# Placing TensorE's short matmuls between its long ones in the attention stage of a five-stage fp32 kernel

## The chip, the cores and the metric

The program runs on one core of a Trainium2 chip. The metric is the device time of one execution in microseconds; the kernel before was run three times. Hardware numbers in this text come from its profile.

## The reference, cut to what is computed

Five layers work in turn on x of shape (4, 512, 128): a gated feed-forward, a state-space mixer, the feed-forward again, a mixture of experts, attention with 8 heads, and the experts again. Each stands behind a layer norm and is added to x. The change touches attention alone:

```python
q = (x @ Wq + bq).reshape(Bsz, Tlen, NUM_HEADS, HEAD_DIM)      # 8 heads of 128
kv = x @ Wkv + bkv                                             # one k and one v for all heads
k, v = (kv[..., :HEAD_DIM], kv[..., HEAD_DIM:])
q = q + pe[None, None, :, :]                                   # after a transpose to (b, h, t, d)
k = k + pe[None, :, :]
scores = jnp.einsum('bhqd,bkd->bhqk', q, k) * scale
scores = jnp.where(causal[None, None, :, :], scores, jnp.finfo(scores.dtype).min)
probs = jax.nn.softmax(scores, axis=-1)
attn = jnp.einsum('bhqk,bkd->bhqd', probs, v)
return out @ Wo                                                # out: heads side by side
```

## The kernel before, in words

Each engine has its own instruction list, written out by hand, and the lists are tied together by counting semaphores. A layer is a phase that all engines enter together. Attention is phase 4. It goes over 4 blocks of 512 tokens (one sequence each) and, within a block, over 8 heads; the first three blocks are a loop (`Fori`), the last is written out.

An fp32 product is made of three matmuls on split operands (`mm3`, L227: hi x hi, hi x lo, lo x hi), which the engine runs at one column per cycle. Of one head, TensorE (`att_pe`, L1219 to L1344) does:

- `score(i, h)`, L1247: four row tiles of 128 queries, in the order 3, 2, 0, 1 (`ORDER`, L1200). Row tile r has three matmuls of 128(r+1) columns (L1261 to L1263) and a short one that adds the causal mask (L1264). The semaphore `s` goes up after tiles 3, 0 and 1.
- `values(i, h-1)`, L1279: probabilities of the head before, times v, 12 matmuls of 512, 384, 256 and 128 columns (L229 to L231). It waits for `pt_lo` 3g+3, the third low part of the transposed probabilities.
- `q_proj(i, h+2)`, L1239: three matmuls of 512 columns for the queries two heads on. In head 6 it is `k_proj` of the next block, in head 7 the next block's first `q_proj`; in the last block both are left out.
- `out_proj(i, h-2)`, L1292: three matmuls of 512 columns, none in heads 0 and 1.
- `turn(i, h)`, L1268: ten transposes of 128x128 of this head's probabilities (L1276), in the order of `PT_UNITS` (L1207): tile 2 (two transposes), tiles 1 and 3 (four), tile 0 (four). The semaphore `pt` goes up after each of the three. Before them it waits for `p` (all exponentials) and for `pn`: 2 normalised row tiles for the first unit, 4 for the others.

After head 7 come `v_proj` of the next block, `out_proj`(6), `values`(7), `q_proj`(1) and `score` of the next block's head 0, and `out_proj`(7). Head 0 of the loop therefore has no `score` or `values` in front.

ScalarE (`att_act`, L1346) does for each head: four exponentials with row sums (`p`, L1369), the copy of `values` and its high part (L1376, L234), three high parts `pt_hi` of the transposes (L1389), a high part of q. VectorE (`att_dve`, L1410): two reciprocals and four normalisations (L1447, L1451), `q32` out of the projection's bank (L1434), then first `pt_lo`, second `pt_lo`, the minimum of row tile 3 of the next head (L1440), third `pt_lo`, and the minima of tiles 2, 0 and 1. The minimum of tile 3 waits for one `s` of that head, those of tiles 2 and 0 for two, that of tile 1 for three. GpSimd makes the low parts of q, k, v and of the heads' outputs.

Of the kernel before, what the change touches and what calls it, by code (L numbers as in the profile page):

```python
# [1 line left out]

# [5 lines left out]
P = 128  # L17
# [7 lines left out]
HEADS = 8  # L25
# [34 lines left out]
def program(nc, d):  # L60
    ctx = ExitStack()
    with ctx:
# [12 lines left out]
        xn_hi = sb("xn_hi", [P, NT], F32R)  # L75
        xn_lo = sb("xn_lo", [P, NT], F32R)
# [42 lines left out]
        with ExitStack() as layer:  # L119
            lb = keeper(layer)  # L120
            ah, al = lb("ah", [P, NA], F32R), lb("al", [P, NA], F32R)
# [23 lines left out]
            with ExitStack() as s:  # L145
                fb = keeper(s)
                xb_hi, xb_lo = fb("xb_hi", [P, T], F32R), fb("xb_lo", [P, T], F32R)
                k_hi, k_lo = fb("k_hi", [P, T], F32R), fb("k_lo", [P, T], F32R)
# [3 lines left out]
                q_hi, q_lo = fb("q_hi", [P, 2, T], F32R), fb("q_lo", [P, 2, T], F32R)  # L152
                p32 = fb("p32", [P, 4, T])
                pt_hi, pt_lo = fb("pt_hi", [P, 3, T], F32R), fb("pt_lo", [P, 3, T], F32R)
                o_hi, o_lo = fb("o_hi", [P, 2, T], F32R), fb("o_lo", [P, 2, T], F32R)
# [5 lines left out]
        ps = ctx.enter_context(nc.psum_tensor("ps", [P, 8, T], F32))  # L161
# [62 lines left out]
        def cut(b):  # L224
            return slice(b * T, (b + 1) * T)

        def mm3(pe, out, w_hi, w_lo, x_hi, x_lo, start, stop):  # L227

            pe.matmul(out, w_hi, x_hi, start=start, stop=False, skip_group_check=True)  # L229
            pe.matmul(out, w_hi, x_lo, start=False, stop=False, skip_group_check=True)  # L230
            return pe.matmul(out, w_lo, x_hi, start=False, stop=stop, skip_group_check=True)  # L231

        def split_hi(act, hi, full):
            return act.activation(hi, full, ACT.Identity)  # L234
# [967 lines left out]
        def scores_at(r):  # L1202
            bank, lo = S_AT[r]
            return ps[:, bank, lo:lo + P * (r + 1)]
# [5 lines left out]
        def pt_at(kb):  # L1210
            bank, lo = PT_AT[kb]
            return ps[:, bank, lo:lo + T - P * kb]
# [4 lines left out]
            return ps[:, bank, lo:lo + n]  # L1217

        def att_pe(pe, L):  # L1219
            def k_proj(i, blk, first=False):  # L1220
                if not first:
                    pe.wait_ge(*A("q32", 8 * i - 2))
                w = slice(A_K, A_K + P)
                mm3(pe, ps[:, 5, :], ah[:, w], al[:, w], xn_hi[:, blk], xn_lo[:, blk], True, True).then_inc(A["kp"], 1)

            def v_proj(i, x_hi, x_lo, first=False):
                if not first:
                    pe.wait_ge(*A("xb_lo", i))
                    pe.wait_ge(*A("p", 32 * i - 3))
                w = slice(A_V, A_V + P)  # L1230
                for t in range(4):
                    tt = slice(t * P, (t + 1) * P)
                    out = ps[:, 0, tt]
                    pe.matmul(out, x_hi[:, tt], ah[:, w], start=True, stop=False, skip_group_check=True)
                    pe.matmul(out, x_hi[:, tt], al[:, w], start=False, stop=False, skip_group_check=True)
                    last = pe.matmul(out, x_lo[:, tt], ah[:, w], start=False, stop=True, skip_group_check=True)
                last.then_inc(A["vp"], 1)

            def q_proj(i, blk, h):  # L1239
                if h == 0:  # L1240
                    pe.wait_ge(*A("k32", i + 1))
                else:
                    pe.wait_ge(*A("q32", 8 * i + h))
                w = slice(A_Q + h * P, A_Q + (h + 1) * P)
                mm3(pe, ps[:, 5, :], ah[:, w], al[:, w], xn_hi[:, blk], xn_lo[:, blk], True, True).then_inc(A["qp"], 1)

            def score(i, h, first=False):  # L1247
                g = 8 * i + h
                if h == 0:
                    pe.wait_ge(*A("k_lo", i + 1))  # L1250
                    pe.wait_ge(*A("v32", i + 1))
                pe.wait_ge(*A("q_lo", g + 1))
                for k, r in enumerate(ORDER):
                    if not first and r != 0:
                        pe.wait_ge(*A("p", 4 * g - 4 + {3: 1, 2: 3, 1: 4}[r]))
                        if r == 1:
                            pe.wait_ge(*A("pt_lo", 3 * g - 2))
                    n = P * (r + 1)
                    q = slice(r * P, n)
                    out = scores_at(r)  # L1260
                    pe.matmul(out, q_hi[:, h % 2, q], k_hi[:, 0:n], start=True, stop=False, skip_group_check=True)  # L1261
                    pe.matmul(out, q_hi[:, h % 2, q], k_lo[:, 0:n], start=False, stop=False, skip_group_check=True)  # L1262
                    pe.matmul(out, q_lo[:, h % 2, q], k_hi[:, 0:n], start=False, stop=False, skip_group_check=True)  # L1263
                    last = pe.matmul(out[:, r * P:n], idr[:, :], maskr[:, :], start=False, stop=True, skip_group_check=True)  # L1264
                    if r != 2:
                        last.then_inc(A["s"], 1)

            def turn(i, h):  # L1268
                g = 8 * i + h
                pe.wait_ge(*A("p", 4 * g + 4))  # L1270
                pe.wait_ge(*A("pt_lo", 3 * g))
                for tiles, _, _, need in PT_UNITS:
                    pe.wait_ge(*A("pn", 4 * g + need))
                    for kb in tiles:
                        for r in range(kb, 4):
                            last = pe.transpose(pt_at(kb)[:, (r - kb) * P:(r - kb + 1) * P], p32[:, r, kb * P:(kb + 1) * P], ident)  # L1276
                    last.then_inc(A["pt"], 1)

            def values(i, h):  # L1279
                g = 8 * i + h  # L1280
                if h == 0:
                    pe.wait_ge(*A("v_lo", i + 1))
                pe.wait_ge(*A("o32", g))
                pe.wait_ge(*A("pt_lo", 3 * g + 3))
                for kb in range(4):
                    part, lo = PT_PART[kb]
                    n = T - kb * P
                    last = mm3(pe, ps[:, 6, kb * P:T], v_hi[:, kb, :], v_lo[:, kb, :], pt_hi[:, part, lo:lo + n],
                               pt_lo[:, part, lo:lo + n], kb == 0, kb == 3)
                last.then_inc(A["o"], 1)  # L1290

            def out_proj(i, h):  # L1292
                pe.wait_ge(*A("o_lo", 8 * i + h + 1))
                if h == 0:
                    pe.wait_ge(*A("x_new", i))
                w = slice(A_O + h * P, A_O + (h + 1) * P)
                mm3(pe, ps[:, 7, :], ah[:, w], al[:, w], o_hi[:, h % 2, :], o_lo[:, h % 2, :], h == 0, h == HEADS - 1)\
                    .then_inc(A["y"], 1)

            def heads(i, last):  # L1300
                blk, following = bass.ds(i * T, T), bass.ds((i + 1) * T, T)
                for h in range(HEADS):
                    if h:
                        score(i, h)
                        values(i, h - 1)
                    if h < HEADS - 2:
                        q_proj(i, blk, h + 2)
                    elif h == HEADS - 2 and not last:
                        k_proj(i + 1, following)
                    elif not last:  # L1310
                        q_proj(i + 1, following, 0)
                    if h >= 2:
                        out_proj(i, h - 2)
                    turn(i, h)
                if not last:
                    v_proj(i + 1, xb_hi, xb_lo)
                out_proj(i, HEADS - 2)
                values(i, HEADS - 1)
                if not last:
                    q_proj(i + 1, following, 1)  # L1320
                    score(i + 1, 0)
                out_proj(i, HEADS - 1)

            def first_kv(step):

                if step == 0:
                    pe.wait_ge(a_lo, 1)
                    pe.wait_ge(*L("centred", 1))
                    pe.wait_ge(*L("xn_lo", 1))
                    v_proj(0, xn_hi[:, 0:T], xn_lo[:, 0:T], True)  # L1330
                else:
                    pe.wait_ge(*L("normed", 2))
                    k_proj(0, cut(0), True)

            ln_pe(pe, L, first_kv)
            pe.wait_ge(*A("mask", 2))
            banks_free(pe, L)
            q_proj(0, cut(0), 0)
            q_proj(0, cut(0), 1)
            score(0, 0, True)  # L1340
            pe.wait_ge(*L("xn_lo", NB))
            with pe.Fori(0, NB - 1) as i:
                heads(i, False)
            heads(NB - 1, True)  # L1344
# [425 lines left out]
```

## Time and profile before

| | us |
|---|---|
| runs of the kernel before | 1946.06, 1946.1, 1943.2 |
| median | 1946.06 |
| span of the profiled execution | 1940.6 |
| attention stage in it | about 1219 to 1461 |

The profile has one record per instruction. PE is TensorE's matmuls, PEld its weight loads; DVE is VectorE, ACT ScalarE, POOL GpSimd. Starts and durations are in us from the start of the span. A matmul's end is modelled. A row that begins with L and a number is named by the line of the kernel; `ps<-k_hi,q_hi` reads: written to `ps`, the moving operand `k_hi`, the stationary one `q_hi`. "x10" means that ten records of the same kind stand in one row.

### The profile page before, as it was taken

How to read it: one execution, taken by the hardware profiler on the slowest of the kernel's cores; microseconds unless marked ns; L12 is line 12 of the kernel's file. 1: busy time of each engine (PE TensorE's matmuls, PEld its weight loads, DVE VectorE, ACT ScalarE, POOL GpSimd, SP SyncE). 2: the span in 40 equal slices, each digit the busy share in tenths (PEclk: the TensorE clock that was granted, in tenths of full speed). 3: DMA queues.
4: the chain of work that ended last, by engine and by line, in shares of the span. 5: the costliest groups of instructions: out<-in, count | busy, mean ns of one | idle time of the engine just before them, and what ended most of it. 6: DMA issues, size and time to landing. Idle time of an engine off the chain costs nothing.

```text
span 1940.6 us, 26739 instructions
## 1 busy us (share of the span) xinstructions
PE 1710.9 (88%) x7108; PEld 1270.5 (65%) x7108; DVE 1322.9 (68%) x2019; ACT 972.8 (50%) x1864; POOL 910.7 (47%) x786
## 2 busy tenths in 40 slices
PE   6997566666668997899999999899998899999999
PEld 3775322222226774688888887788885688888887
DVE  4555699999985556655555556777784655555565
ACT  3344634333334334455555554677783455555554
POOL 3001057445441003466666665434432466666666
PEclk8998768888889997999999999999997899999999
DMA  2000000000000001000010000000000000010001
GB/s 103 1 0 1 0 0 1 0 0 0 1 0 7 1 1 41 17 27 27 27 32 27 27 27 11 1 1 0 0 1 17 11 27 27 27 32 27 27 27 38
DMA packets 27793, 31.14 MB, mean 16 GB/s; under 512 B 3211, under 2 KB 26211, under 8 KB 27363
## 3 DMA queue, kind: packets, MB, share of 16 engines
q1 hardware_dynamic: 27747, 30.58, 5.2%
q8 instruction: 22, 0.36, 0.1%
q14 instruction: 24, 0.20, 0.0%
HBM read 29.52 MB, written 1.05 MB: 16 GB/s over the span
## 4 chain that ended last, share of the span: by engine, by line
PE 63%; issue 3%; DVE 3%; POOL 3%; ACT 1%; POOLq 0%; DVEq 0%; ACTq 0%
PE ps L229 17%; PE ps L230 16%; PE ps L231 16%; PE ps L914 4%; PE ps L1276 2%; POOL m_hc L837 2%; PE ps L1261 1%; PE ps L1263 1%; PE ps L1262 1%; PE ps L1264 0%; DVE r_t L1126 0%; POOL e_lo L237 0%; PE ps L251 0%; PE ps L264 0%; PE ps L258 0%
## 5 line engine op out<-in xcount | busy, mean ns | idle before, releaser
L237 POOL TENSOR_TENSOR e_lo<-e_h,e_hi 128x512 fp32r<-128x512 f32 (+1 forms) x368 | 479.4, 1303 | 313.3 <-ACT e_hi L234 313.3
L1157 DVE TENSOR_TENSOR e_p<-e_s,ps 128x512 f32<-128x512 f32 x352 | 242.1, 688 | 285.9 <-PE ps L231 195.4
L979 ACT ACTIVATE e_s<-ps 128x512 f32<-128x512 f32 (+1 forms) x368 | 220.6, 599 | 392.7 <-PE ps L231 392.6
L627 PE MATMUL ps<-m_hc,const 128*128 128x512 f32 x256 | 183.2, 806 | 113.6 <-POOL m_hc L837 105.4
L230 PE MATMUL ps<-xn_lo,eh 128*128 128x512 f32 x704 | 279.1, 397 | 0.0
L229 PE MATMUL ps<-xn_hi,eh 128*128 128x512 f32 x704 | 278.7, 396 | 0.0
L837 POOL TENSOR_TENSOR m_hc<-m_h,m_c 128x512 f32<-128x512 f32 x128 | 181.1, 1419 | 204.0 <-DVE m_h L793 164.7
L1166 DVE TENSOR_TENSOR e_h<-e_p,ps 128x512 f32<-128x512 f32 x352 | 242.3, 688 | 49.7 <-DVE e_p L1157 18.1
L231 PE MATMUL ps<-xn_hi,el 128*128 128x512 f32 x704 | 274.9, 390 | 0.0
L234 ACT ACTIVATE e_hi<-e_h 128x512 fp32r<-128x512 f32 (+1 forms) x368 | 229.6, 624 | 24.0 <-DVE e_h L1070 21.7
L793 DVE TENSOR_TENSOR_SCAN m_h<-ln_t,ln_c 128x512 f32<-128x512 f32 x128 | 237.8, 1858 | 0.5 <-ACT ln_t L701 0.5
L237 POOL TENSOR_TENSOR xn_lo<-ln_c,xn_hi 128x512 fp32r<-128x512 f32 (+1 forms) x24 | 34.2, 1427 | 325.8 <-ACT xn_hi L234 325.7
L627 PEld LDWEIGHTS ps<-m_hc,const 128*128 128x128 f32 x256 | 48.0, 230 | 207.8 <-POOL m_hc L837 195.4
L229 PEld LDWEIGHTS ps<-xn_hi,eh 128*128 128x128 f32 x704 | 132.7, 189 | 32.0 <-DVE e_p L1157 1.3
L230 PEld LDWEIGHTS ps<-xn_lo,eh 128*128 128x128 f32 x704 | 132.7, 189 | 31.4
L231 PEld LDWEIGHTS ps<-xn_hi,el 128*128 128x128 f32 x704 | 132.9, 189 | 30.9
L701 ACT ACTIVATE ln_t<-m_raw,neg_a 128x512 f32<-128x512 f32 x128 | 90.6, 719 | 121.9 <-DVE m_h L793 112.4
L229 PE MATMUL ps<-e_hi,eh 128*128 128x512 f32 x352 | 139.5, 396 | 1.9 <-POOL e_lo L237 1.9
L231 PE MATMUL ps<-e_hi,el 128*128 128x512 f32 x352 | 140.1, 398 | 0.0
L914 PE MATMUL ps<-rwt,eh 128*128 128x512 f32 x352 | 137.2, 390 | 1.4 <-ACT rwt L1000 1.4
L230 PE MATMUL ps<-e_lo,eh 128*128 128x512 f32 x352 | 136.3, 387 | 0.0
L229 PE MATMUL ps<-hid_hi,wh 128*128 128x512 f32 x288 | 122.2, 424 | 7.2 <-DVE hid_lo L237 6.2
(242 smaller groups left out, 3392.2 us busy)
## 6 DMA issues: line engine op xcount, KB each, us to landing
e_raw<-in_experts SPq DMA_DIRECT2D x88, 192.0 KB, 2.3
e_raw<-in_pick SPq DMA_DIRECT2D x88, 64.0 KB, 2.0
w_raw<-in_ffn SPq DMA_DIRECT2D x1, 1280.0 KB, 10.4
a_raw<-in_attn SPq DMA_DIRECT2D x1, 1152.0 KB, 5.2
w_raw<-in_ffn SPq DMA_DIRECT2D x1, 1024.0 KB, 7.8
out<-x SPq DMA_DIRECT2D x4, 256.0 KB, 2.4
x<-in_x SPq DMA_DIRECT2D x1, 768.0 KB, 4.6
w_raw<-in_ffn SPq DMA_DIRECT2D x1, 512.0 KB, 5.8
```

Of the source, the lines that this page charges most:

```text
L229: pe.matmul(out, w_hi, x_hi, start=start, stop=False, skip_group_check=True)
L230: pe.matmul(out, w_hi, x_lo, start=False, stop=False, skip_group_check=True)
L231: return pe.matmul(out, w_lo, x_hi, start=False, stop=stop, skip_group_check=True)
L234: return act.activation(hi, full, ACT.Identity)
L237: return eng.tensor_tensor(lo, full, hi.bitcast(F32), ALU.subtract)
L627: pe.matmul(ps[:, 4 + m, :], ident, m_hc[:, q % DEEP, :], start=(n == 0), stop=(n == DS - 1), skip_group_check=True).then_inc(M["y_sum"], 1)
L793: dve.tensor_tensor_scan(m_h[:, q % DEEP, :], m_da[:, q % DEEP, :], m_db[:, q % DEEP, :], 0.0, ALU.mult, ALU.add).then_inc(M["h"], 1)
L837: pool.tensor_tensor(m_hc[:, q % DEEP, :], m_h[:, q % DEEP, :], m_c[:, n % 2, :], ALU.mult).then_inc(M["hc"], 1)
L914: pe.matmul(ps[:, 6 + j % 2, :], eh[:, c, 3, :], rwt[:, cut(b)], start=True, stop=True).then_inc(S["spread"], 1)
L979: act.activation(e_s[0:rows_, buf, :], ps[0:rows_, 4, :], ACT.Silu).then_inc(S["silu"], 1)
L1157: dve.tensor_tensor(e_p[0:rows_, buf % 2, :], e_s[0:rows_, buf, :], ps[0:rows_, 5, :], ALU.mult).then_inc(S["gated"], 1)
L1166: dve.tensor_tensor(e_h[:, j % 4, :], e_p[:, j % 2, :], ps[:, 6 + j % 2, :], ALU.mult).then_inc(S["weighted"], 1)
```

## The change

`score` is written anew: the three products of tile 0 are placed between those of tile 3, then the two causal matmuls follow, then tile 2, then tile 1. `s` goes up after tiles 3, 2 and 1. `k_proj`, `q_proj` and `out_proj` are taken apart into single matmuls (`product`), and the transposes are placed between them: two projection products, transpose, third projection product, transpose, output product, transpose, output product, transpose, output product, and then the other six. The order of the transposes is now tile 2 (two), tile 3, tile 1 (three), tile 0 (four), with `pt` going up after the second, sixth and tenth as before. The waits for `p`, `pt_lo` and `pn` 2 stand behind the second projection product, the wait for `pn` 4 behind the second output product. The other engines' programs are unchanged.

```diff
+        def product(pe, k, out, w_hi, w_lo, x_hi, x_lo, start, stop):
+
+            return pe.matmul(out, w_lo if k == 2 else w_hi, x_lo if k == 1 else x_hi, start=start and k == 0,
+                             stop=stop and k == 2, skip_group_check=True)
...
-                for k, r in enumerate(ORDER):
-                    if not first and r != 0:
-                        pe.wait_ge(*A("p", 4 * g - 4 + {3: 1, 2: 3, 1: 4}[r]))
-                        if r == 1:
-                            pe.wait_ge(*A("pt_lo", 3 * g - 2))
...
-                    if r != 2:
-                        last.then_inc(A["s"], 1)
...
+                if not first:
+                    pe.wait_ge(*A("p", 4 * g - 1))
+                for k in range(3):
+                    part(3, k)
+                    part(0, k)
+                causal(3).then_inc(A["s"], 1)
+                causal(0)
+                for k in range(3):
+                    part(2, k)
+                causal(2).then_inc(A["s"], 1)
+                if not first:
+                    pe.wait_ge(*A("p", 4 * g))
+                    pe.wait_ge(*A("pt_lo", 3 * g - 2))
+                for k in range(3):
+                    part(1, k)
+                causal(1).then_inc(A["s"], 1)
...
-                    if h < HEADS - 2:
-                        q_proj(i, blk, h + 2)
-                    elif h == HEADS - 2 and not last:
-                        k_proj(i + 1, following)
-                    elif not last:
-                        q_proj(i + 1, following, 0)
-                    if h >= 2:
-                        out_proj(i, h - 2)
-                    turn(i, h)
...
+                    projection(h, 0)
+                    projection(h, 1)
+                    pe.wait_ge(*A("p", 4 * g + 4))
+                    pe.wait_ge(*A("pt_lo", 3 * g))
+                    pe.wait_ge(*A("pn", 4 * g + 2))
+                    turn(i, h, 2, 2)
+                    projection(h, 2)
+                    turn(i, h, 2, 3).then_inc(A["pt"], 1)
+                    output(h, 0)
+                    turn(i, h, 3, 3)
+                    output(h, 1)
+                    pe.wait_ge(*A("pn", 4 * g + 4))
+                    turn(i, h, 1, 1)
+                    output(h, 2)
+                    turn(i, h, 1, 2)
+                    turn(i, h, 1, 3).then_inc(A["pt"], 1)
+                    for r in range(3):
+                        turn(i, h, 0, r)
+                    turn(i, h, 0, 3).then_inc(A["pt"], 1)
```

## Rows read from the trace of the kernel before

**Rows 1.** The page: the span, and busy time by engine.
```profile
span 1940.6 us, 26739 instructions
PE 1710.9 (88%) x7108; PEld 1270.5 (65%) x7108; DVE 1322.9 (68%) x2019; ACT 972.8 (50%) x1864; POOL 910.7 (47%) x786
```
**Rows 2.** Table by stretches: length, busy by engine with counts, PEclk, DMA share, GB/s.
```profile
1239.00:1280.00 41.00, 41.00 (x271) 37.66 (x270) 33.52 (x86) 32.42 (x84) 15.19 (x13) 1.00 0.01 2
```
**Rows 3.** Timeline of weight loads, one head (start, duration, what).
```profile
1244.83 0.19 PEld L1262 LDWEIGHTS ps<-k_lo,q_hi 128*128 128x128 f32 x1
...
1245.29 0.19 PEld L1264 LDWEIGHTS ps<-maskr,idr 128*128 128x128 f32 x1
1245.52 0.19 PEld L1261 LDWEIGHTS ps<-k_hi,q_hi 128*128 128x128 f32 x1
1245.63 0.19 PEld L1262 LDWEIGHTS ps<-k_lo,q_hi 128*128 128x128 f32 x1
1245.81 0.19 PEld L1263 LDWEIGHTS ps<-k_hi,q_lo 128*128 128x128 f32 x1
1245.98 0.19 PEld L1264 LDWEIGHTS ps<-maskr,idr 128*128 128x128 f32 x1
...
1246.95 0.19 PEld L1264 LDWEIGHTS ps<-maskr,idr 128*128 128x128 f32 x1
1247.16 0.19 PEld L229 LDWEIGHTS ps<-pt_hi,v_hi 128*128 128x128 f32 x1
...
1249.40 0.19 PEld L231 LDWEIGHTS ps<-xn_hi,al 128*128 128x128 f32 x1
```
**Rows 4.** Timeline of PE: the ten transposes ahead of that head's score.
```profile
1243.73 1.25 PE L1276 MATMUL ps<-const,p 128*128 128x128 f32 x10
```
**Rows 5.** Timeline of DVE over the same head.
```profile
1245.22 0.69 DVE L237 TENSOR_TENSOR pt_lo<-ps,pt_hi 128x512 fp32r<-128x512 f32 x1 [0.23 <-ACT pt_hi L1389]
1245.83 0.68 DVE L1440 TENSOR_REDUCE st<-ps 128x1 f32<-128x512 f32 x1
1246.42 0.68 DVE L237 TENSOR_TENSOR pt_lo<-ps,pt_hi 128x512 fp32r<-128x512 f32 x1
...
1248.71 0.82 DVE L1451 TENSOR_SCALAR p<-p,st 128x512 f32<-128x512 f32 x2
...
1249.63 0.55 DVE L1451 TENSOR_SCALAR p<-p,st 128x128 f32<-128x128 f32 x2
...
1252.04 0.69 DVE L237 TENSOR_TENSOR pt_lo<-ps,pt_hi 128x512 fp32r<-128x512 f32 x1 [0.23 <-ACT pt_hi L1389]
```
**Rows 6.** Timelines of PE and DVE, first score of block 2.
```profile
1343.00 0.22 PE L1264 MATMUL ps<-maskr,idr 128*128 128x128 f32 x1
...
1344.03 0.27 PE L1264 MATMUL ps<-maskr,idr 128*128 128x128 f32 x1
...
1344.34 1.09 DVE L1440 TENSOR_REDUCE st<-ps 128x1 f32<-128x384 f32 x3 [0.39 <-PE ps L1264]
```
**Rows 7.** Timeline of PE: transposes of heads 1, 0 (block 2) and 6 (last block).
```profile
1236.70 1.46 PE L1276 MATMUL ps<-const,p 128*128 128x128 f32 x10
...
1347.55 0.44 PE L1276 MATMUL ps<-const,p 128*128 128x128 f32 x2 [1.34 <-DVE p L1451]
1348.21 1.09 PE L1276 MATMUL ps<-const,p 128*128 128x128 f32 x8 [0.22 <-DVE p L1451]
...
1446.95 1.39 PE L1276 MATMUL ps<-const,p 128*128 128x128 f32 x10
```
**Rows 8.** Timelines of DVE and PEld: first and last of the 28 places.
```profile
1233.26 0.68 DVE L237 TENSOR_TENSOR pt_lo<-ps,pt_hi 128x512 fp32r<-128x512 f32 x1
1234.00 0.19 PEld L229 LDWEIGHTS ps<-pt_hi,v_hi 128*128 128x128 f32 x1
...
1449.77 0.68 DVE L237 TENSOR_TENSOR pt_lo<-ps,pt_hi 128x512 fp32r<-128x512 f32 x1
1450.57 0.19 PEld L229 LDWEIGHTS ps<-pt_hi,v_hi 128*128 128x128 f32 x1
```

More of the change, by code:

```diff
@@ L1219, in att_pe, with k_proj @@
         def att_pe(pe, L):
-            def k_proj(i, blk, first=False):
-                if not first:
+            def k_proj(i, blk, k, first=False):
+                if k == 0 and not first:
                     pe.wait_ge(*A("q32", 8 * i - 2))
                 w = slice(A_K, A_K + P)
-                mm3(pe, ps[:, 5, :], ah[:, w], al[:, w], xn_hi[:, blk], xn_lo[:, blk], True, True).then_inc(A["kp"], 1)
+                mm = product(pe, k, ps[:, 5, :], ah[:, w], al[:, w], xn_hi[:, blk], xn_lo[:, blk], True, True)
+                if k == 2:
+                    mm.then_inc(A["kp"], 1)
             def v_proj(i, x_hi, x_lo, first=False):
@@ L1237, in v_proj, with q_proj @@
                 last.then_inc(A["vp"], 1)
-            def q_proj(i, blk, h):
-                if h == 0:
+            def q_proj(i, blk, h, k):
+                if k == 0 and h == 0:
                     pe.wait_ge(*A("k32", i + 1))
-                else:
+                elif k == 0:
                     pe.wait_ge(*A("q32", 8 * i + h))
                 w = slice(A_Q + h * P, A_Q + (h + 1) * P)
-                mm3(pe, ps[:, 5, :], ah[:, w], al[:, w], xn_hi[:, blk], xn_lo[:, blk], True, True).then_inc(A["qp"], 1)
+                mm = product(pe, k, ps[:, 5, :], ah[:, w], al[:, w], xn_hi[:, blk], xn_lo[:, blk], True, True)
+                if k == 2:
+                    mm.then_inc(A["qp"], 1)
             def score(i, h, first=False):
@@ L1252, in score @@
                 pe.wait_ge(*A("q_lo", g + 1))
-                for k, r in enumerate(ORDER):
-                    if not first and r != 0:
-                        pe.wait_ge(*A("p", 4 * g - 4 + {3: 1, 2: 3, 1: 4}[r]))
-                        if r == 1:
-                            pe.wait_ge(*A("pt_lo", 3 * g - 2))
[L1258 to L1264, printed above, removed]
-                    if r != 2:
-                        last.then_inc(A["s"], 1)
@@ L1268, in turn, with part @@
[L1268 to L1277, printed above, removed]
+                def part(r, k):
+                    q = slice(r * P, (r + 1) * P)
+                    x_lo, y_lo = (k == 2), (k == 1)
+                    pe.matmul(scores_at(r), (q_lo if x_lo else q_hi)[:, h % 2, q], (k_lo if y_lo else k_hi)[:, 0:P * (r + 1)],
+                              start=(k == 0), stop=False, skip_group_check=True)
@@ new lines, in causal @@
+                def causal(r):
+                    return pe.matmul(scores_at(r)[:, r * P:(r + 1) * P], idr[:, :], maskr[:, :], start=False, stop=True, skip_group_check=True)
+                if not first:
[7 more added lines that the diff above has]
+                    part(2, k)
@@ L1279, in values, with turn @@
+                causal(2).then_inc(A["s"], 1)
[5 more added lines that the diff above has]
+                causal(1).then_inc(A["s"], 1)
+            def turn(i, h, kb, r):
+                return pe.transpose(pt_at(kb)[:, (r - kb) * P:(r - kb + 1) * P], p32[:, r, kb * P:(kb + 1) * P], ident)
             def values(i, h):
@@ L1290, in values, with out_proj, projection, output @@
                 last.then_inc(A["o"], 1)
-            def out_proj(i, h):
-                pe.wait_ge(*A("o_lo", 8 * i + h + 1))
-                if h == 0:
+            def out_proj(i, h, k):
+                if k == 0:
+                    pe.wait_ge(*A("o_lo", 8 * i + h + 1))
+                if k == 0 and h == 0:
                     pe.wait_ge(*A("x_new", i))
                 w = slice(A_O + h * P, A_O + (h + 1) * P)
-                mm3(pe, ps[:, 7, :], ah[:, w], al[:, w], o_hi[:, h % 2, :], o_lo[:, h % 2, :], h == 0, h == HEADS - 1)\
-                    .then_inc(A["y"], 1)
+                mm = product(pe, k, ps[:, 7, :], ah[:, w], al[:, w], o_hi[:, h % 2, :], o_lo[:, h % 2, :], h == 0, h == HEADS - 1)
+                if k == 2:
+                    mm.then_inc(A["y"], 1)
             def heads(i, last):
                 blk, following = bass.ds(i * T, T), bass.ds((i + 1) * T, T)
+                def projection(h, k):
+                    if h < HEADS - 2:
+                        q_proj(i, blk, h + 2, k)
+                    elif h == HEADS - 2 and not last:
+                        k_proj(i + 1, following, k)
+                    elif not last:
+                        q_proj(i + 1, following, 0, k)
+                def output(h, k):
+                    if h >= 2:
+                        out_proj(i, h - 2, k)
                 for h in range(HEADS):
+                    g = 8 * i + h
                     if h:
@@ L1305, in heads @@
                         values(i, h - 1)
-                    if h < HEADS - 2:
-                        q_proj(i, blk, h + 2)
-                    elif h == HEADS - 2 and not last:
-                        k_proj(i + 1, following)
-                    elif not last:
-                        q_proj(i + 1, following, 0)
-                    if h >= 2:
-                        out_proj(i, h - 2)
-                    turn(i, h)
+                    projection(h, 0)
[17 more added lines that the diff above has]
+                    turn(i, h, 0, 3).then_inc(A["pt"], 1)
                 if not last:
                     v_proj(i + 1, xb_hi, xb_lo)
-                out_proj(i, HEADS - 2)
+                for k in range(3):
+                    out_proj(i, HEADS - 2, k)
                 values(i, HEADS - 1)
                 if not last:
-                    q_proj(i + 1, following, 1)
+                    for k in range(3):
+                        q_proj(i + 1, following, 1, k)
                     score(i + 1, 0)
-                out_proj(i, HEADS - 1)
+                for k in range(3):
+                    out_proj(i, HEADS - 1, k)
             def first_kv(step):
@@ L1332, in first_kv @@
                     pe.wait_ge(*L("normed", 2))
-                    k_proj(0, cut(0), True)
+                    for k in range(3):
+                        k_proj(0, cut(0), k, True)
             ln_pe(pe, L, first_kv)
@@ L1337, in att_pe @@
             banks_free(pe, L)
-            q_proj(0, cut(0), 0)
-            q_proj(0, cut(0), 1)
+            for h in range(2):
+                for k in range(3):
+                    q_proj(0, cut(0), h, k)
             score(0, 0, True)
```

## The prediction

> **What bounds the kernel now.** I read the page first for the size of things: the span is 1940.6 us and TensorE is busy 88% of it [rows 1]. Only the attention stage is edited, some 240 us from 1219 to 1461. The table by stretches then shows that in 41 us of its steady part PE is busy for 41.00 us at full clock [rows 2]. Read alone, this says that TensorE's own work sets the time. It has to be checked, because the end of a matmul is modelled and a matmul stretched by a wait also shows as busy.
>
> So the third view is the timeline of one head by its weight loads, which are the better clock: each load starts when the matmul before it starts. In [rows 3], a long matmul (512 columns, L below) takes 0.23 us: 1245.29 to 1245.52. A short one (128 columns, S below) takes 0.11 us in a run of its own kind: the ten transposes start at 1243.73 [rows 4] and the first score starts with the load at 1244.83 [rows 3], so 1.10 us for ten. Now the same rows at `values`: its first load is at 1247.16, while the last causal matmul, whose load is at 1246.95, began at about 1247.07 (a 256-column one of 0.12 us runs before it), when an unhindered load would have started. PE lost 0.09 us there, and the "busy" record hides it. What was late? VectorE's timeline [rows 5]: the third `pt_lo` runs from 1246.42 to 1247.10, and the load starts 0.06 after its end (0.12 in the last block, below). The chain before it is gapless: second `pt_lo` 1245.22, minimum of row tile 3 at 1245.83, third `pt_lo` 1246.42, paces 0.61 and 0.59. In [rows 8] the first and the last of the 28 such places (7 heads of 4 blocks) read the same way: 1233.26 + 0.68 then 1234.00; 1449.77 + 0.68 then 1450.57. So a steady head is a loop of two parts: from `values` to the sixth transpose PE is the bound, from there to the next `values` it is ScalarE and VectorE, with PE 0.09 us behind that. The head takes 6.82 us (second `pt_lo` at 1245.22 and one head later at 1252.04, [rows 5]).
>
> **The change, part by part.**
>
> **1. Shorts between longs: no gain.** The meant saving is that the load of an S hides behind an L. A short streams in well under 0.11 us, so its 0.11 is the load of the next weights. The kernel before already holds an S between two Ls: the causal matmul between 512- and 384-column scores. It starts with the load at 1245.52. The next load starts at 1245.63 (that of the second 384-column product), and then the 384s come at 1245.81 and 1245.98, 0.17 each [rows 3]. From 1245.52 to 1245.81 is 0.29 for S plus a 384; less 0.17 or 0.18, the S still costs 0.11. Its own load was hidden behind the L, but the load of the L behind it can only begin when the S begins, and lasts 0.11. An S costs 0.11 whatever stands before it. The matmuls, their shapes and number are unchanged, so this part is 0. Bounds: -0.055 us for each S with an L on both sides (three in a score, four in a block of transposes), and 0.
>
> The Trainium skill, "TensorE: Matmul & The Clock Gate", section "Step-by-step: what each phase is for", speaks for the change: it says that the engine's reorder window pulls weight loads ahead of matmuls in flight. The trace agrees for one load ahead, and shows none pulled two ahead. Were the rule enough by itself, the seven shorts would give back what rival B below counts.
>
> **2. Score order: the signal for row tile 3 comes later.** Before, `s` for tile 3 is raised by the fourth matmul of the score (3 L, causal), now three products of tile 0 lie in front: 3 x 0.11 = 0.33 us later. By load clock the score starts at 1244.83 and the causal matmul at 1245.52; it would start at 1245.85. Where VectorE was idle, its minimum started 0.04 after the end of the causal record (1344.03 + 0.27, then 1344.34, [rows 6]); behind an L that record is 0.22 long, as the earlier pair of the same rows has it. So the minimum would start at 1245.85 + 0.26 = 1246.11 in place of 1245.83: 0.28 later (0.05 of slack covers the rest). Queued behind this minimum on VectorE is the third `pt_lo`, and `values` waits for that, with no slack left at all. So all 0.28 lands on PE as a longer stop in front of `values`. Bounds: 0.12 (if the three shorts cost 0.055 each) and 0.33 (no slack). 28 places x 0.28 = +7.8 us. The later tiles don't suffer: tile 2's causal matmul moves to where tile 0's stood, and VectorE reaches these minima after the third `pt_lo` anyway. Tile 0 now raises no `s`, and its minimum comes after tile 2's.
>
> In the first head of a block the same delay costs nothing: no `pt_lo` lies between the minima, and VectorE is idle for a while before the second minimum.
>
> **3. Transposes start four longs earlier.** Before, all of the projection (3 L) and the output product (3 L) stood before the wait on `pn`. Now only two products do. The projection's second product starts at 1249.40 [rows 3], so PE would want the transpose's weights at 1249.40 and the transpose at 1249.63. The two normalisations it waits for end at 1248.71 + 0.82 = 1249.53 [rows 5], and the load follows by 0.06 as above: 1249.59, with 0.11 for the load 1249.70. A new stop of 0.06 us. VectorE's chain from the third `pt_lo` on hangs on nothing that moved, so this holds in the slower loop also. Queued behind the waiting transpose are the last projection product and the output product. `q32` waits for the former and comes some 0.15 later on VectorE, but it ends some 0.9 before the second `pt_lo` behind it, which waits for `pt_hi` until 1252.04 [rows 5]; the first, of half the size, fits between them, so this is covered. 22 heads (h 2 to 7 in three blocks, h 2 to 5 in the last) x 0.06 = +1.3 us. Bounds 0 and 0.12: after a stop in [rows 7] a pair of transposes takes 0.44, which is 0.06 more than the 0.38 (0.11 + 0.27) of a running pair. The second wait, on `pn` 4 (1249.63 + 0.55 + 0.06 = 1250.24, [rows 5]), comes two Ls and three Ss later, and would want its weights at about 1250.49: no stop.
>
> **4. Heads with less cover.** In h 0 PE stops for `pn` twice now: the two transposes at 1347.55, eight at 1348.21, 0.66 apart [rows 7]. The last projection product and one more transpose now stand between the waits, so after the second only seven shorts are left: about -0.1. The same in h 1, where ten transposes take 1.46 instead of 1.25 [rows 7, 4]. Four blocks x (0.09 + 0.07) = -0.6. In h 6 and 7 of the last block there is no projection: the output product's 3 L covered the wait (ten transposes in 1.39, a stop of 0.14, [rows 7]). Now the first transpose stands directly behind `values`: it could start at 1249.40 - 0.23 = 1249.17 by the times of the head above and gets its weights for 1249.70: a stop of 0.53, less the 0.14 saved, +0.4 each, +0.8 together.
>
> **5. What costs nothing.** The moved `y` and `qp` signals have a head of slack; the earlier first `pt` frees ScalarE sooner, but the second `pt`, which carries the loop, still has four shorts behind it. No DMA moves, and SP and POOL's orders are untouched.
>
> **Sum:** 0 + 7.8 + 1.3 - 0.6 + 0.8 = +9.3 us. A steady head goes from 6.82 to about 7.16. On the profiled execution that is 1940.6 to 1949.9; the median of the runs stands 5.5 us above that span, and the same difference on it is 1946.1 + 9.3 = **1955.4 us**.
>
> **Rivals.** **A, the forecast** (loads not hidden, signal late): chance 0.65. **B, the loads are hidden and the gain is lost elsewhere:** the S between Ls costs 0.055. Then the score's saving doesn't count, since VectorE's chain ends last: its signal comes 0.17 late, 0.12 net, at `values`. Four transposes save 0.22 and the stop of 0.06 stays: -0.04 per head, -1 us with part 4: 1945. For it: the meant mechanism. Against: [rows 3]. Chance 0.12. **C, the other side:** shorts are hidden and the minimum's delay isn't on the path, because VectorE isn't truly the releaser of `values` and that 0.09 is PE's own cost of a wait. Place: the start of `values`. Price: seven shorts x 0.055 less 0.06 = -0.33 a head, about -9 us: 1937. It decides for faster from the point where the signal's delay counts for less than 0.1 us. Against it: the fixed distance after `pt_lo` at 28 places. Chance 0.08. **D, more stops:** the waits that now stand in the middle of the block (`pn` 2, `o_lo`, `pn` 4) each cost PE 0.06 to 0.09, the size of its stops at a wait in [rows 7] and [rows 3], in place of one 0.06: 22 heads x 0.12 to 0.21 more, 1958 to 1960. Chance 0.15; against it, `o_lo` and `q32` are waited for in the kernel before too, with no gap in PE's records [rows 2].
>
> **How the numbers follow.** The range holds A, B and D and leaves out C and sums with both ends of parts 2 and 3 (28 x 0.05 and 22 x 0.06 more than D): 1944.5 to 1960. A measurement tells some 0.2% (3.9 us) from no change. Faster by over that: C, 0.08, and a little of B: 0.09. Within: the rest of B and a little of A, 0.14. Slower: 0.77.
>
> **What the profile after would show.** Right: the first load of `values` still 0.06 after the third `pt_lo`, heads of 7.1 to 7.2 us, minimum of tile 3 about 1.28 after the score's start in place of 1.00; S and L between each other taking 0.34 a pair. Wrong, if a pair takes 0.29 (part 1), if the minimum isn't later (part 2), or if the first transpose's load starts with the second projection product (part 3).

## The result and the profile after

The changed kernel takes 1952.35 us in the median of 13 runs; the kernel before, run beside it, 1942.15 us (13 runs). The ratio is 1.0053, 95% interval 1.0039 to 1.0068: +10.3 us by the ratio, where +9.3 was forecast; the interval runs from +7.6 to +13.2. The level of the kernel before in these runs is 4 us under that of the three runs shown first, so the comparison goes by the ratio and not by 1955.4.

The page of the profiled execution after, and the same 41 us of the steady part as in [rows 2]:

```profile
span 1946.0 us, 26739 instructions
PE 1710.2 (88%) x7108; PEld 1264.0 (65%) x7108; DVE 1325.5 (68%) x2019; ACT 970.4 (50%) x1864; POOL 911.2 (47%) x786
...
1239.00:1280.00 41.00, 40.18 (x259) 35.14 (x258) 32.84 (x81) 30.62 (x80) 14.08 (x12) 1.00 0.01 1
```

The spans differ by 5.4 us only, because what stands ahead of attention took some 3 us less in the second of these two executions (the first score began at 1223.7 before and at 1220.6 after), though nothing there was edited. From the first score's matmul to the last output product's matmul it is 238.0 us before and 246.9 after: +8.9. That stretch is called "the stage" below. In the same 41 us the profile has 259 matmuls of TensorE instead of 271, at full clock in both.

Weight loads of one head after (compare [rows 3]; "x2" is a long one and a short one 0.11 behind it), then VectorE over the same head (compare [rows 5]):

```profile
1249.13 0.30 PEld L1257 LDWEIGHTS ps<-k_hi,q_hi 128*128 128x128 f32 x2
1249.48 0.30 PEld L1257 LDWEIGHTS ps<-k_lo,q_hi 128*128 128x128 f32 x2
1249.82 0.30 PEld L1257 LDWEIGHTS ps<-k_hi,q_lo 128*128 128x128 f32 x2
1250.16 0.30 PEld L1261 LDWEIGHTS ps<-maskr,idr 128*128 128x128 f32 x2
...
1251.37 0.19 PEld L1261 LDWEIGHTS ps<-maskr,idr 128*128 128x128 f32 x1
1251.87 0.19 PEld L220 LDWEIGHTS ps<-pt_hi,v_hi 128*128 128x128 f32 x1 [0.31 <-DVE pt_lo L233]
1251.98 0.19 PEld L221 LDWEIGHTS ps<-pt_lo,v_hi 128*128 128x128 f32 x1
```
```profile
1249.63 0.69 DVE L233 TENSOR_TENSOR pt_lo<-ps,pt_hi 128x512 fp32r<-128x512 f32 x1 [0.74 <-ACT pt_hi L1424]
1250.53 0.69 DVE L1475 TENSOR_REDUCE st<-ps 128x1 f32<-128x512 f32 x1 [0.20 <-PE ps L1261]
1251.14 0.68 DVE L233 TENSOR_TENSOR pt_lo<-ps,pt_hi 128x512 fp32r<-128x512 f32 x1
...
1253.42 0.82 DVE L1486 TENSOR_SCALAR p<-p,st 128x512 f32<-128x512 f32 x2
...
1256.78 0.69 DVE L233 TENSOR_TENSOR pt_lo<-ps,pt_hi 128x512 fp32r<-128x512 f32 x1 [0.74 <-ACT pt_hi L1424]
```

Three things are to be seen. A pair of long and short takes 0.34 us (1249.48, 1249.82, 1250.16), which is 0.23 + 0.11: nothing is hidden. VectorE now idles 0.20 us ahead of the minimum of tile 3, released by the causal matmul (L1261 here), which begins at 1250.27, with the second load of the row at 1250.16; in [rows 5] it came to it straight from `pt_lo`. And the first load of `values` (1251.87) still follows the end of the third `pt_lo` (1251.14 + 0.68 = 1251.82), but 0.50 us after the last causal load instead of 0.21 in [rows 3]; unhindered it is 0.12 (experiment 3). The list of waits, which before had no such row for TensorE in the stage, has one now (engine and line, released by: us in total, times, longest). Since the ends of matmuls are modelled, its total is less than the time lost:

```profile
PE ps L220 <- DVE pt_lo L233: 5.5, 29, 0.3
```

Time from the first load of `values` of one head to that of the next, in us, by block. A head's number is that of the later `values`; the first block's and the last block's are shown, the two between are like the first within 0.02. The step from `values` of head 7 to that of the next block's head 0 is 11.99 to 12.06 before and 12.17 to 12.25 after. "Steady heads" below are heads 2 to 6 of the three blocks in the loop. In the last block, which is written out, the load of `values` follows `pt_lo` by 0.12 us instead of 0.05, and its heads 2 to 5 are some 0.06 longer in both kernels.

| | 1 | 2 | 3 | 4 | 5 | 6 | 7 |
|---|---|---|---|---|---|---|---|
| before, first block | 6.34 | 6.82 | 6.82 | 6.82 | 6.82 | 6.82 | 6.29 |
| after, first block | 6.53 | 7.15 | 7.15 | 7.15 | 7.16 | 7.16 | 6.33 |
| before, last block | 6.34 | 6.88 | 6.90 | 6.90 | 6.90 | 6.34 | 5.74 |
| after, last block | 6.53 | 7.22 | 7.20 | 7.20 | 7.20 | 6.97 | 6.07 |

### The profile page after: what moved, and what is told of

Read it like the earlier page. It is cut to its first block, busy times and chain, and to the rows that moved or that the text cites. A ratio compares the mean times of both kernels' runs of the same rounds, so it can differ in the third digit from the quotient of the medians.

```text
span 1946.0 us, 26739 instructions
## 1 busy us (share of the span) xinstructions
PE 1710.2 (88%) x7108; PEld 1264.0 (65%) x7108; DVE 1325.5 (68%) x2019; ACT 970.4 (50%) x1864; POOL 911.2 (47%) x786
## 4 chain that ended last, share of the span: by engine, by line
PE 61%; DVE 4%; issue 4%; POOL 3%; ACT 1%; POOLq 0%; DVEq 0%; ACTq 0%
PE ps L220 16%; PE ps L221 16%; PE ps L222 16%; PE ps L910 4%; PE ps L226 2%; PE ps L1257 2%; PE ps L1281 2%; POOL m_hc L833 2%; DVE pt_lo L233 1%; PE ps L247 0%; DVE r_t L1122 0%; POOL e_lo L233 0%; PE ps L260 0%; DVE st L1475 0%; PE ps L254 0%
```

## The experiments

The 13 times of the kernel before spread over 11 us, those of the others over 8 to 14, so the verdicts rest on the length of a steady head and of the stage. Each kernel left one trace. How well the two lengths repeat can be read only from pairs of kernels in which nothing on the path differs: heads of 6.82 and 6.82 to 6.83, stages of 238.0 and 238.0 (the kernel before and experiment 8), heads of 6.73 and 6.73, stages of 236.0 and 235.9 (experiments 3 and 6). Experiments 5, 6, 7, 8 and 9 were timed once each (1941.40, 1942.62, 1941.07, 1936.55 and 1942.12 us), which tells nothing against that spread; only their traces are used.

**1 and 2. The change in two halves.** The new score alone:

```diff
-                for k, r in enumerate(ORDER):
...
+                for k in range(3):
+                    part(3, k)
+                    part(0, k)
+                causal(3).then_inc(A["s"], 1)
+                causal(0)
...
```

> Only the new order of the score (tile 0's products between those of tile 3, the signal after tile 2 in place of tile 0); projections, output products and transposes stand as before. Theory A (the later signal for row tile 3 is on the path through VectorE's minimum and third pt_lo): minimum of tile 3 at 1.28 us after the score's start in place of 1.00, 28 steady heads of 6.82 become 7.10 to 7.11, +8 us, so some 85% of what the whole change costs. Rival M (the loss comes from mixing matmuls as such, on TensorE itself, or from the waits set in the block of transposes): heads stay within 0.1 of 6.82, under +3 us.

Measured: 1952.91 us, ratio 1.0044 (1.0027 to 1.0060). Steady heads 7.13, stage 246.6, +8.7 of the +8.9. One head:

```profile
1246.79 0.69 DVE L1452 TENSOR_REDUCE st<-ps 128x1 f32<-128x512 f32 x1 [0.20 <-PE ps L1261]
1247.40 0.68 DVE L237 TENSOR_TENSOR pt_lo<-ps,pt_hi 128x512 fp32r<-128x512 f32 x1
...
1248.13 0.19 PEld L229 LDWEIGHTS ps<-pt_hi,v_hi 128*128 128x128 f32 x1 [0.31 <-DVE pt_lo L237]
```

The new block of transposes alone, the score in its old order:

```diff
-                    turn(i, h)
...
+                    projection(h, 0)
+                    projection(h, 1)
...
+                    turn(i, h, 2, 2)
+                    projection(h, 2)
...
```

> Only the transposes are placed between projection and output products; the score has its old order. Theory A: steady heads 6.82 plus 0.03 to 0.06, heads 6 and 7 of the last block some 0.4 longer, heads 0 and 1 some 0.1 shorter; in all +1 to +2 us. Rival M: most of the +9 is here, heads of 7.0 or more. If a load could hide behind a long one after all, heads would be 6.6.

Measured: 1941.89 us, ratio 1.0000 (0.9985 to 1.0015). Steady heads 6.83 to 6.87, stage 238.3, +0.3, under the expected +1 to +2. Each part has the expected sign, and each loss is at the low end of what was expected or under it: 6.23 in place of 6.34 for head 1, 11.89 in place of 12.01 for the step to the next block; against this stand +0.32 and +0.33 in heads 6 and 7 of the last block. Mixed transposes as such don't cost much, then: nearly all of the loss is in the half that moves a signal. But that half mixes too, in the score, and only experiment 9 parts the two there.

**3 and 4. VectorE's order, the link in the chain.** If `values` is late because its `pt_lo` is queued behind the minimum of tile 3, then exchanging these two sets it free, in either kernel:

```diff
-                        if h + 1 < HEADS and unit:
-                            minima(i, h + 1, ORDER[0:1] if unit == 1 else ORDER[1:])
+                        if h + 1 < HEADS and unit == 2:
+                            minima(i, h + 1)
```

On the kernel before:

> The kernel before, with one thing changed on VectorE: the third pt_lo stands before the minimum of row tile 3 of the next head, not behind it. Theory A: the stop of 0.09 in front of values goes away (pt_lo ends some 0.5 before it is wanted), steady heads 6.73 in place of 6.82; heads with little cover get later probabilities (0.1 to 0.2 in heads 1 and the last two); in all -1 to -3 us. If the 0.09 is TensorE's own cost of a wait, heads stay at 6.82.

Measured: steady heads 6.73, stage 236.0, -2.0; time 1939.99 us, ratio 0.9992 (0.9976 to 1.0007), which the timing can't tell from 1. The two `pt_lo` now run as a pair, and the loads at `values` keep the pace of the run, 0.12 after the causal load where [rows 3] had 0.21:

```profile
1242.82 1.29 DVE L237 TENSOR_TENSOR pt_lo<-ps,pt_hi 128x512 fp32r<-128x512 f32 x2 [0.35 <-ACT pt_hi L1389]
...
1244.55 0.19 PEld L1264 LDWEIGHTS ps<-maskr,idr 128*128 128x128 f32 x1
1244.67 0.19 PEld L229 LDWEIGHTS ps<-pt_hi,v_hi 128*128 128x128 f32 x1
```

So the 0.09 us was no price of a wait on TensorE itself, which rival C of the prediction needed.

On the changed kernel:

> The changed kernel with the same exchange on VectorE: the minimum of tile 3, and so its late signal, no longer stands between values and its pt_lo. Theory A: values starts without a stop, 0.29 + 0.09 us earlier in each of 28 heads, but the probabilities are ready later against it, and the first transpose, which now stands early, stops TensorE for some 0.2: heads of about 6.95 to 7.0 in place of 7.15, +3 to +6 us against the kernel before in place of +10. Rival M (mixing itself is the cost): heads stay at 7.1 or more.

Measured: 1945.93 us, ratio 1.0021 (1.0006 to 1.0036), stage 238.7, steady heads 6.83 to 6.87. The direction holds; heads of 7.1 or more, as rival M has it, are out. In the loop the size is better than expected, 6.85 against 6.95 to 7.0. The first transpose does stop TensorE there:

```profile
1248.02 0.19 PEld L226 LDWEIGHTS ps<-xn_lo,ah 128*128 128x128 f32 x1
1248.49 0.14 PEld L1281 LDWEIGHTS ps<-const,p 128*128 128x128 f32 x1 [0.28 <-DVE p L1486]
...
1248.68 0.14 PEld L1281 LDWEIGHTS ps<-const,p 128*128 128x128 f32 x1
```

From the first of these loads, with which the first projection product starts, to the last, with which the third starts, it is 0.66 us. In the changed kernel it is 0.60, without a stop (1253.90 to 1254.50). So TensorE is stopped for 0.06 here, and for 0.06 to 0.09 in the steady heads, where 0.2 was expected. In the last block the same stretch takes 0.81 us (1424.22 to 1425.03), a stop of 0.2, and heads 2 to 5 there take 6.95 to 6.99. The stage gives +0.7 us, the times give +4.1 (+1.2 to +7.0 by the interval), so the time grew more than the stage; where the rest lies is not shown.

**5. A short between longs, in a loop that TensorE alone bounds.** Three transposes between and behind the output products, on the kernel of experiment 3:

```diff
+                    output(h, 0)
...
+                    pe.wait_ge(*A("pn", 4 * g + 2))
+                    turn(i, h, 2, 2)
+                    output(h, 1)
+                    turn(i, h, 2, 3).then_inc(A["pt"], 1)
+                    output(h, 2)
+                    turn(i, h, 3, 3)
+                    pe.wait_ge(*A("pn", 4 * g + 4))
...
```

> On the kernel with the third pt_lo first on VectorE (steady head 6.73, TensorE never stopped in it): three transposes are moved between and behind the three output products, late enough that their probabilities are ready; the score has its old order. So a short between two long ones stands in a loop that TensorE alone bounds. Theory A (a short costs 0.11 whatever stands before it, since the load behind it can't begin earlier): 6.73 to 6.75. Rival B (its load hides): two to three times 0.055 less, 6.57 to 6.62.

Measured: steady heads 6.74 to 6.76, stage 235.7. Two longs with a short between them:

```profile
1258.71 0.14 PEld L1269 LDWEIGHTS ps<-const,p 128*128 128x128 f32 x1
1258.94 0.19 PEld L226 LDWEIGHTS ps<-o_lo,ah 128*128 128x128 f32 x1
1259.08 0.14 PEld L1269 LDWEIGHTS ps<-const,p 128*128 128x128 f32 x1
1259.29 0.19 PEld L226 LDWEIGHTS ps<-o_hi,al 128*128 128x128 f32 x1
```

The transpose begins at 1258.94, and so does the load of the long behind it; the next transpose's load can start 0.14 later, the next transpose begins at 1259.29: 0.35 us for the pair. Rival B is out, and a pair of a product and a transpose even costs some 0.005 to 0.01 more than its two parts, which is most of the 0.01 to 0.03 by which this head is over 6.73.

**6. What the 0.11 is.** The causal matmuls move 64 columns in place of 128, on the kernel of experiment 3:

```diff
-                    last = pe.matmul(out[:, r * P:n], idr[:, :], maskr[:, :], start=False, stop=True, skip_group_check=True)
+                    last = pe.matmul(out[:, r * P:r * P + 64], idr[:, :], maskr[:, 0:64], start=False, stop=True, skip_group_check=True)
```

> On the kernel with the third pt_lo first on VectorE (6.73 us, bound by TensorE): each causal matmul moves 64 columns in place of 128, which leaves out the mask on half of each diagonal block. Four shorts a head stream half as long. Theory A (the next weight load is their price): no change, 6.73. Rival (they are bound by their columns): 4 x 0.027 less, 6.62.

Measured: 6.73, stage 235.9. The one between two longs, load by load:

```profile
1245.19 0.19 PEld L1264 LDWEIGHTS ps<-maskr,idr 128*128 128x128 f32 x1
1245.42 0.19 PEld L1261 LDWEIGHTS ps<-k_hi,q_hi 128*128 128x128 f32 x1
1245.52 0.19 PEld L1262 LDWEIGHTS ps<-k_lo,q_hi 128*128 128x128 f32 x1
1245.70 0.19 PEld L1263 LDWEIGHTS ps<-k_hi,q_lo 128*128 128x128 f32 x1
```

It begins at 1245.42 and the long behind it at 1245.52, 0.11 later before rounding, as with 128 columns (1245.52 and 1245.63 in [rows 3]). The columns that it moves aren't its price. The Trainium skill, "TensorE: Matmul & The Clock Gate", section "LDWEIGHTS (loading the stationary operand)", says that a load takes its number of columns divided by 1.2 (in ns); 128 columns give an estimate of 107 ns, and the rows here have 0.10 to 0.11. By that rule no order of the matmuls can bring a short under a load, unless two loads could wait in the array; no run here shows that they can. No run here loads fewer than 128 columns for a short either, so that the price is the load, and not some other fixed price of a load and a matmul, is not shown. The argument needs only that it is 0.11 in every place.

**7. How far the signal moves.** One of tile 0's three products ahead of tile 3's causal matmul:

```diff
...
+                    for k in range(3):
+                        if r != 0 or k >= 1:
+                            part(r, k)
+                        if r == 3 and k < 1:
+                            part(0, k)
...
```

In this kernel a part of tile 0's scores is lost from the sum, most likely its first product, since tile 2 starts in the same bank before tile 0 is finished; all instructions run, and the time is that of the full work.

> The kernel before with one of tile 0's three products moved ahead of tile 3's causal matmul (the other two stay behind tile 2). Theory A: the signal comes 0.11 later, 0.05 of it is slack, so steady heads grow by 0.06 to 0.08, to 6.88 to 6.90, against 7.13 with three moved. If the loss came from rewriting the order as such (banks, accumulation of two tiles side by side) it would be a third of 0.31, 6.92.

Measured: 6.90 to 6.93, stage 240.4. That is +0.09, between the two expectations and 0.01 from either, so the length alone tells nothing apart. VectorE's rows do:

```profile
1248.84 0.69 DVE L237 TENSOR_TENSOR pt_lo<-ps,pt_hi 128x512 fp32r<-128x512 f32 x1 [0.23 <-ACT pt_hi L1395]
1249.52 0.69 DVE L1446 TENSOR_REDUCE st<-ps 128x1 f32<-128x512 f32 x1
1250.13 0.68 DVE L237 TENSOR_TENSOR pt_lo<-ps,pt_hi 128x512 fp32r<-128x512 f32 x1
```

The minimum follows the second `pt_lo` by 0.68 us instead of the 0.61 of [rows 5], and the third `pt_lo` follows the minimum by 0.61 instead of 0.59. So of the 0.12 by which the signal is later, about 0.045 is slack, as [rows 5] and [rows 6] had suggested; some 0.075 reaches the minimum, 0.01 more comes from the pace of the two instructions behind it, and that is nearly all of the +0.09. With none, one and three products ahead, the head takes 6.82, 6.91 and 7.13: each costs its 0.11 from the second on.

**8. The signal in its old place, the rest of the score's order new.** On experiment 1, tile 3's causal matmul ahead of tile 0's products:

```diff
                 for k in range(3):
                     part(3, k)
-                    part(0, k)
                 causal(3).then_inc(A["s"], 1)
+                for k in range(3):
+                    part(0, k)
                 causal(0)
```

> The new tile order 3, 0, 2, 1 of the score with its signals after 3, 2 and 1, but tile 3's causal matmul and signal come before tile 0's three products; VectorE as in the kernel before. Theory A: only the place of the first signal counts, heads of 6.82. If the order of the tiles or the two later signals had a part in the loss, heads between 6.9 and 7.13.

Measured: 6.82 to 6.83, stage 238.0, as before. So neither the order of the tiles nor the two later signals have a part in the loss. Tile 0's products no longer stand between those of tile 3 here, so what mixing them costs is left to 9.

**9. The late signal without the link.** Experiment 1 with VectorE's exchange:

> The new score order alone (as in the kernel that showed heads of 7.13), with one exchange on VectorE: the third pt_lo ahead of the minimum of tile 3. Nothing differs on TensorE from the kernel with 7.13. Theory A (the late signal costs only because values waits through this minimum): heads of 6.73 to 6.75, as without the new score order. Rival M (side-by-side accumulation or the mixed order costs TensorE itself): 7.0 or more.

Measured: 6.74 to 6.76, stage 236.2, so mixing the score costs 0.01 to 0.03 over the 6.73 of experiment 3. The score is that of the 7.13 us head, mixed as before, and `values` starts without a stop:

```profile
1244.39 1.29 DVE L237 TENSOR_TENSOR pt_lo<-ps,pt_hi 128x512 fp32r<-128x512 f32 x2 [0.23 <-ACT pt_hi L1401]
1245.60 1.67 DVE L1452 TENSOR_REDUCE st<-ps 128x1 f32<-128x512 f32 x4
...
1246.13 0.19 PEld L1261 LDWEIGHTS ps<-maskr,idr 128*128 128x128 f32 x1
1246.25 0.19 PEld L229 LDWEIGHTS ps<-pt_hi,v_hi 128*128 128x128 f32 x1
```

Together with 8 this settles where the loss comes from. Taking away either the signal's delay or the place where it is waited for takes away the loss, while every matmul of the new score stays.

**10. What is worth keeping.** VectorE's exchange, the old score, and the mixed block only in heads 0 and 1, where TensorE waits for probabilities anyway:

```diff
+                    if h > 1:
+                        for k in range(3):
+                            projection(h, k)
+                        for k in range(3):
+                            output(h, k)
...
+                        continue
                     projection(h, 0)
                     projection(h, 1)
...
```

> The best of the parts: the third pt_lo first on VectorE, the score in its old order, and the transposes placed between the projection products only in heads 0 and 1 of each block, where TensorE waits for probabilities anyway. Theory A: steady heads 6.73; from values of head 0 to that of head 1 6.24 in place of 6.35, from head 7 to head 0 some 0.1 less; the stage some 235.2 us against 238.0 before and 236.0 with VectorE's exchange alone: -3 us, -0.15%, at the edge of what the timing tells. Rival M (mixing costs): not under 236.0.

Measured: steady heads 6.73, head 1 in 6.24, the step to the next block 11.80, stage 235.6; 1939.11 us, ratio 0.9986 (0.9973 to 0.9999). It is some 2.7 us faster than the kernel before by the ratio, whose interval only just leaves out 1, and 2.4 by the stage, where -3 was expected; it beats the changed kernel by some 11 us in the stage. Against experiment 3, the exchange alone, it gains 0.4 us of stage; the times of the two can't be told apart.

## Why the prediction was right

**Part 1, no gain from mixing: right**, and shown, not only argued: pairs of 0.34 in the changed kernel, 0.35 in experiment 5, and a half-size short at the full price in experiment 6. It came from 32 causal matmuls that already stood between longs. The sum had 0 here. In the score that is what was measured; a product with a transpose costs 0.005 to 0.01 more than apart, counted under part 3.

**Part 2, the late signal: right in place and size.** The minimum starts 1.29 us after the score (1250.53 less 1249.24, the second load of the row at 1249.13, which starts with the score), against 1.00 before and 1.28 forecast. It starts 0.26 after the causal matmul (1250.27), as forecast, though the forecast took that from a causal matmul behind a long one and the new order has it behind a short one. The half that holds it costs +8.7 us of stage, where the term was +7.8: a head grew by 0.31, not by 0.28. In the means over the steady heads of experiment 1, 0.29 is the minimum's delay, 0.01 the slower pace from the minimum to the third `pt_lo` (0.61 instead of 0.60), and 0.01 lies in TensorE's own part of the head.

**Part 3, a stop of 0.06 at the first transpose: the step was mis-sized.** The mechanism was there, the price wasn't:

```profile
1253.90 0.19 PEld L226 LDWEIGHTS ps<-xn_lo,ah 128*128 128x128 f32 x1
1254.29 0.14 PEld L1281 LDWEIGHTS ps<-const,p 128*128 128x128 f32 x1 [0.20 <-DVE p L1486]
1254.36 0.19 PEld L226 LDWEIGHTS ps<-xn_hi,al 128*128 128x128 f32 x1
...
1254.13 0.39 PE L226 MATMUL ps<-xn_lo,ah 128*128 x1
1254.36 0.28 PE L1281 MATMUL ps<-const,p 128*128 128x128 f32 x1
```

The transpose's load did wait for `pn` (1253.42 + 0.82 + 0.05 = 1254.29), 0.16 after the projection product began at 1254.13. But the transpose then began 0.07 after its load, at 1254.36, which is just when the product before it was through (1254.13 + 0.23). The forecast had it wait 0.11 for its weights (and by its own numbers, 1249.70 less 1249.63, the stop would have been 0.07, not 0.06). So the stop is nothing. The heads of experiment 2 are still 0.03 over 6.82: the stretch from the first projection product to the next score takes 2.50 us there instead of 2.47, most of it the four pairs at 0.005 to 0.01. Over the 22 heads this adds up to +0.6 us, where part 3 had +1.3 and part 1 nothing.

**Part 4, little cover: right in sign.** Heads 0 and 1 gained about 0.11 each in experiment 2, where 0.09 and 0.07 stood: -0.9 instead of -0.6. Heads 6 and 7 of the last block lost 0.32 and 0.33 instead of 0.4 each: +0.65 instead of +0.8.

The halves add up: 8.7 + 0.3 = 9.0 against 8.9 for the stage. That the sum, +9.3, came so near is partly luck: part 2 was 0.9 too small, parts 3 and 4 together 1.1 too large. The interval of the times, +7.6 to +13.2, holds the stage's +8.9 and is too wide to judge single terms. Of the rivals, B fell with experiment 5, C with experiments 3 and 9, D with experiment 2: its place, the waits within the block of transposes, should have cost 0.12 to 0.21 more a head, and the block got 0.02 to 0.03 longer in all.

## What to carry to other kernels

Before work is moved into a run of instructions, ask which semaphore stands behind that run and who is queued behind the one who waits for it; three matmuls of 0.11 us ahead of a signal cost 0.31 us a head although their engine did no more work. An engine whose records show no gap may still be waiting at each round; the distance from another engine's end to its next weight load, 0.05 us in the 21 places of the loop and 0.12 in the seven of the last block, gave it away. And before an order is built that is meant to hide a load, look for one instance of the pattern in the old trace: here the causal matmul between two longs already cost its full 0.11.

## What the runs showed that I had not expected

In the changed kernel a transpose begins 0.07 us after the start of its weight load, with the load's record still open (0.14 long), and the next load starts with it; in a run, loads follow each other only every 0.11. So here a late load of a short matmul cost less than its pace suggests: 0.16 us late was made up in full. The first long matmul of `values`, late in the same way, made up nothing: it began 0.11 after its load, with the next load at 1251.98.
